# Gate logits of a four-expert block: weights stationary in four column tiles, tokens streaming, and the logits turned back

## What is computed

```python
xn = _modulate(_ln(x), sh_mlp, sc_mlp)                     # 32 x 128 tokens of 144 channels
xf = xn.reshape(-1, C)
gate_logits = xf @ w_gate                                  # w_gate: 144 x 4
topk_logits, topk_idx = jax.lax.top_k(gate_logits, 2)
gates = jax.nn.softmax(topk_logits, axis=-1)
cw = sum(one_hot(topk_idx, 4) * gates[..., None], axis=1)  # token x expert, two of four not zero
hmid = gelu(einsum('tc,ech->eth', xf, w1) + b1)            # all four experts, 576 hidden units each
eo = einsum('eth,ehc->etc', hmid, w2) + b2
moe = einsum('te,etc->tc', cw, eo)
x = x + g_mlp * moe
```

## Time and profile before

| | us |
|---|---|
| median of 3 runs | 1564.3 (1563.18 to 1565.5) |
| span of the profiled execution, first to last instruction | 1547.8 |
| run median less that span | 16.5 |
| TensorE matmul busy | 1415.6 (91%) |
| DVE busy | 1036.5 (67%) |
| ACT busy | 778.5 (50%) |
| POOL busy | 542.2 (35%) |

### The profile page before, as it was taken

How to read it: one execution, slowest core, us unless ns; L and a number is a source line. 1 busy time by engine, 2 the same in 40 slices (tenths; PEclk the granted TensorE clock), 3 DMA queues, 4 the chain that set the end, 5 groups by cost and what they waited for, 6 DMA issues and landing times. The chain is left out here.

```text
span 1547.8 us, 41007 instructions
## 1 busy us (share of the span) xinstructions
PE 1415.6 (91%) x15976; PEld 1065.0 (69%) x15976; DVE 1036.5 (67%) x2592; ACT 778.5 (50%) x1287; POOL 542.2 (35%) x739
## 2 busy tenths in 40 slices
PE   5799988999999998999899778877999799999998
PEld 2377776777777776777676656766777577767776
DVE  4688885766676667888537689887446466666342
ACT  2377763333333335767645456665544266555543
POOL 3355532211131313555323423443335244343322
PEclk9799999999999999999999889999999899999999
DMA  4765631111122032565000333443116667775021
GB/s 129 149 163 147 161 88 52 51 44 44 35 58 75 19 94 62 144 150 138 20 31 22 104 95 104 109 115 104 33 36 86 114 102 109 138 138 97 24 55 47
DMA packets 209128, 134.92 MB, mean 87 GB/s; under 512 B 142461, under 2 KB 191320, under 8 KB 202730
## 3 DMA queue, kind: packets, MB, share of 16 engines
q1 hardware_dynamic: 188978, 129.74, 35.4%
q10 hardware_dynamic: 19960, 2.57, 1.2%
HBM read 98.24 MB, written 33.24 MB: 85 GB/s over the span
## 5 line engine op out<-in xcount | busy, mean ns | idle before, releaser
L1534 DVE TENSOR_REDUCE negm<-banks 128x8 bf16<-128x1024 f32 x256 | 311.1, 1215 | 79.0 <-PE banks L648 77.2
L1223 ACT ACTIVATE prob<-banks 128x1024 f32<-128x1024 f32 x256 | 262.3, 1025 | 194.0 <-PE banks L670 193.3
L1351 ACT ACTIVATE hid<-banks 128x512 f32<-128x512 f32 x144 | 85.9, 597 | 230.5 <-PE banks L951 230.5
L1954 POOL TENSOR_TENSOR X<-X,gx 128x288 f32<-128x288 f32 x128 | 104.7, 831 | 256.9 <-DVE gx L1564 255.1
L967 PEld LDWEIGHTS banks<-wfc,hid 128*128 128x128 f32 x1152 | 157.0, 190 | 30.0 <-issue 19.9
L666 PE MATMUL banks<-qk 54*128 54x128 bf16 (+1 forms) x2048 | 169.4, 236 | 5.7 <-ACT prob L1223 5.0
L670 PE MATMUL banks<-mT,identb 64*128 64x128 bf16 x2048 | 166.2, 225 | 0.3 <-issue 0.3
L967 PE MATMUL banks<-wfc,hid 128*128 128x144 f32 x1152 | 161.4, 286 | 0.0
L648 PE MATMUL banks<-qk 54*128 54x128 bf16 (+1 forms) x2048 | 123.3, 242 | 39.8 <-DVE negm L1534 24.9
L950 PE MATMUL banks<-hT,wfc 128*128 128x512 f32 x288 | 149.1, 599 | 1.7 <-DMA wfc<-in_L_cond_w 1.2
L1725 DVE TENSOR_TENSOR hid<-hid,qk 128x512 f32<-128x512 f32 x128 | 88.9, 695 | 88.8 <-ACT hid L1351 80.4
(11 more groups left out here) (165 smaller groups left out, 2799.2 us busy)
## 6 DMA issues: line engine op xcount, KB each, us to landing
qk<-qk_scr SPq DMA_DIRECT2D x96, 216.0 KB
gbuf<-gate_scr SPq DMA_DIRECT2D x64, 288.0 KB, 4.3
qk_scr<-parts SPq DMA_DIRECT2D x48, 288.0 KB, 2.7
qk<-qk_scr SPq DMA_DIRECT2D x96, 144.0 KB
qk<-cw_scr SPq DMA_DIRECT2D x8, 1024.0 KB, 4.7
qk_scr<-parts SPq DMA_DIRECT2D x48, 144.0 KB, 2.5
qk<-qk_scr SPq DMA_DIRECT2D x96, 72.0 KB
qk<-tok_scr SPq DMA_DIRECT2D x32, 216.0 KB
```

The lines of the kernel that those rows point to most:

```text
L1223: act.activation(prob[:, 2 * (U % 3):2 * (U % 3) + 2, :], pairs[1][:], ACT.Exp, scale=scale).then_inc(a_exp, 1)
L1534: dve.tensor_reduce(negm[:, u // 2, :, 4 * (u % 2):4 * (u % 2) + 4], pairs[0][:].rearrange("q s (h k) -> q s h k", k=T), AX.X, ALU.max, ne ...
L1954: pool.tensor_tensor(x, x, gx[:, q, :, :], ALU.add).then_inc(g_x, 1)
```

## The change

`gate_logits` exchanges the roles of its operands. The four columns of `wgate` become the stationary operand and the 128 tokens of a sequence move. The four sequences' products go to partitions 0, 32, 64 and 96 of the bank, 4 rows and 128 columns each. All four `hT` products are issued first, then the four `hr` products, which now run in float32 over all 66 rows (`rgate` gets two more rows, of zeros).

The logits then have tokens along the columns. A new `logits_out` on DVE copies the bank's 128x128 region to SBUF (`glog`, which reuses the room of `ss`), a new `turn_logits` on TensorE transposes it into columns 128 to 255 of the bank, and `top2` reads there, four of each 32 columns.

The order changes with it. In the expert steps `logits_out` stands at j = 8 and `turn_logits` at j = 9; the parts of `top2` go to j = 10, 11, 12, 14, and `turn_weights` and `copy_weights` to j = 15. In the attention `logits_out` stands at (6, 7), `turn_logits` at (7, 0), and the parts of `top2` at (7, 0), (7, 1), (7, 2), (7, 3); `turn_weights` and `copy_weights` stay at (7, 5) and (7, 6).

```diff
-        rgate = sb("rgate", [REM - 2, E], F32R)
+        rgate = sb("rgate", [REM, E], F32R)
+        glog = ss[:].rearrange("t b h -> t (b h)")
...
                 for b in range(G):
-                    out, at = bank[o][:, E * b:E * b + E], slice(T * b, T * b + T)
-                    pe.matmul(out, hT[:, h, at], wgate[:], start=True, stop=False)
-                    mm = pe.matmul(out, hr[0:REM - 2, h, at], rgate[:], start=False, stop=True)
+                    out, at = bank[o][32 * b:32 * b + E, 0:T], slice(T * b, T * b + T)
+                    pe.matmul(out, wgate[:], hT[:, h, at], start=True, stop=False)
+                for b in range(G):
+                    out, at = bank[o][32 * b:32 * b + E, 0:T], slice(T * b, T * b + T)
+                    mm = pe.matmul(out, rgate[:].bitcast(F32), hr[:, h, at].bitcast(F32), start=False, stop=True)
                 mm.then_inc(s_lg, 1)
+
+            def turn_logits(g, o):
+                pe.wait_ge(d_gl, CR + g + 1)
+                pe.transpose(bank[o][:, T:2 * T], glog[:], ident[:]).then_inc(s_gl, 1)
...
+                        if l == 0 and (g, u) == (7, 0):
+                            turn_logits(0, 6)
...
-                        if g < 7 and j == 14:
+                        if g < 7 and j == 9:
+                            turn_logits(g + 1, 0)
+                        if g < 7 and j == 15:
                             turn_weights(g + 1, 0)
...
-                        if l == 0 and (g, u) in ((6, 7), (7, 0), (7, 1), (7, 3)):
-                            top2(0, {7: 0, 0: 1, 1: 2, 3: 3}[u], 6)
+                        if l == 0 and (g, u) in ((7, 0), (7, 1), (7, 2), (7, 3)):
+                            top2(0, u, 6)
+                        if l == 0 and (g, u) == (6, 7):
+                            logits_out(0, 6)
...
+            def logits_out(g, o):
+                dve.wait_ge(s_lg, CR + g + 1)
+                if g:
+                    dve.wait_ge(s_gl, CR + g)
+                dve.tensor_copy(glog[:], bank[o][:, 0:T]).then_inc(d_gl, 1)
...
-                lv = bank[o][:, 0:G * E].rearrange("t (b e) -> t b e", e=E)
+                lv = bank[o][:, T:2 * T].rearrange("t (b x) -> t b x", b=G)[:, :, 0:E]
...
-                    dve.wait_ge(s_lg, CR + g + 1)
+                    dve.wait_ge(s_gl, CR + g + 1)
...
-                        if g < 7 and j in (9, 10, 11, 13):
-                            top2(g + 1, min(j - 9, 3), 0)
-                        if g < 7 and j == 14:
+                        if g < 7 and j == 8:
+                            logits_out(g + 1, 0)
+                        if g < 7 and j in (10, 11, 12, 14):
+                            top2(g + 1, min(j - 10, 3), 0)
+                        if g < 7 and j == 15:
                             copy_weights(g + 1, 0)
...
+                dve.memset(rgate[REM - 2:REM].bitcast(F32), 0.0)
```

More of the change, by code:

```diff
@@ L265, in build @@
         s_mod, d_ms = sem("s_mod"), sem("d_ms")
+        s_gl, d_gl = sem("s_gl"), sem("d_gl")
         block = ctx.enter_context(nc.Block())
@@ L543, in _ @@
             for x in (s_ada, s_ht, s_hr, s_qk, s_qt, s_v, s_sm, s_mt, s_st, s_pv, s_otok, s_ont, s_onr, s_pj, s_fc1,
-                      s_y, s_lg, s_vt, s_mod, s_k, s_ct):
+                      s_y, s_lg, s_vt, s_mod, s_k, s_ct, s_gl):
                 pe.sem_inc(x, CR)
@@ L1412, in _ @@
             for x in (d_set, d_wa, d_ws, d_mod, d_stat, d_mv, d_hm, d_hr, d_r1, d_sm, d_mt, d_rec, d_on, d_onr, d_gate,
-                      d_ss, d_nw, d_qn, d_top, d_cw, d_y, d_rep, d_xn, d_ms, d_hg, d_bi, d_ct):
+                      d_ss, d_nw, d_qn, d_top, d_cw, d_y, d_rep, d_xn, d_ms, d_hg, d_bi, d_ct, d_gl):
                 dve.sem_inc(x, CR)
@@ L1425, in split_chunk @@
                 st = stage[0:rows, staged(i), 0:n]
-                out = rgate[:] if what == "gate" else SPLIT[what][:, slot(what, k), :]
+                out = rgate[0:rows] if what == "gate" else SPLIT[what][:, slot(what, k), :]
                 dve.wait_ge(d_ws, CR + (i if i < EARLY else i + 1))
```

## The result

The kernel after took 1551.08 us, median of 15 runs (1541.48 to 1557.92); the kernel before took 1563.67 in its 15 runs beside them (1557.37 to 1575.01). The ratio is 0.991, interval 0.9891 to 0.993.

The account below looks back on a forecast made before the run. TensorE was taken to bound the expert layer, a chain of waits the attention's end. 8.9 + 1.0 + 0.4 - 0.4 = 9.9 us off 1564.3 gave 1554.4 us, range 1551.5 to 1560.5.

Parts of the forecast that it names:

- The gate call, 2.05 to 0.65 us: TensorE's gate products: 2.05 us a call before; after, two sets at 0.25 us plus 0.15 for entering the mode.
- The value product of the earlier trace: Attention's float32 product L682 in four column tiles, 0.25 us a set, taken as the price of the new gate products.
- The turn, 0.13 us: The added float32 transpose of the logits on TensorE: 0.13 us a call, bounds 0.1 to 0.3.
- the wait for DVE's copy: TensorE waiting at `turn_logits` for the copy-out: 0.2 us in each of groups 3 and 5, 0.4 in all.
- The `cw` waits of groups 4 and 6, 1.0 us: TensorE's wait at `turn_weights` for DVE's `cw`: 0.5 us goes in each of two groups, bounds 0 and 1.0 in all.
- The late expert weights: Next group's weights read 2.2 us later, 0.4 us left in group 4: nothing charged; slower rival, 1569 us, 4%.
- The first group, +0.4: Gate at the attention's end: 1.2 us saved, nearly all absorbed by DVE waiting for POOL; bounds -1.0 and +1.5.
- the load of the last expert weights under cover: SP's last load of expert weights, behind DVE's `gated` at the attention's end, was said to have cover until 249.56.
- the rival on the clock: The clock fall after the first gate disappears, attention's end gains 1.5 us instead of 0.4: 1552 us; chance 6%.
- The runs lie 16.5 us above that span, and I let that stand: Step from profiled span to run time: the 16.5 us between 1547.8 and 1564.3 were kept unchanged for the new kernel.

Follow-up runs that it names:

- The order alone: The kernel before with only the new order of `top2`, `turn_weights` and `copy_weights`, old gate products kept: 1561.45 us, ratio 0.9991 to before.
- before again: The kernel before, unchanged, run and profiled once more: 1563.33 us, ratio 0.9991 to the other runs of before.
- the first group as before: The kernel after, with the old products and old `top2` places for the first group's gate only: 1554.95 us, ratio 0.9924 to before.
- after again: The kernel after, unchanged, run and profiled once more: 1554.45 us, ratio 0.9946 to before.
- two parts together: The kernel after, with part 2 of the first group's `top2` moved behind part 1 at (7, 1): 1550.58 us, ratio 0.9915 to before.
- old form twice: The kernel before with the 12 instructions of each gate call issued twice: 1596.94 us, ratio 1.0233 to before.
- new form eight times: The kernel after with the 16 instructions of each gate call issued eight times: 1579.85 us, ratio 1.0119 to before.
- four times: The kernel after with the 16 instructions of each gate call issued four times: 1558.73 us, ratio 0.996 to before.
- spread extras: The kernel after with the old products twice more per group, one sequence at each of tiles 10 to 13, result unread: 1580.36 us.

## Why the prediction was right, and where its size was off

**The gate call, 2.05 to 0.65 us: right, but for 0.09 us.** It is 0.55 us to the next product, plus the 0.10 us that this product is slower, plus 0.09 us ahead of the call that the sum did not have: 0.74 in all. The value product of the earlier trace rows was the right row, to 0.03 us a set. The first call, in the attention, took 0.88 us, 0.25 of it an idle stretch. The kernel without column tiles shows the other price, 0.11 us an instruction, to be what it would have been without overlap. The rule of the Trainium skill that was weighed (TensorE: Matmul & The Clock Gate, "Part 3: Packing small matmuls — row/col tiling"), that a weight load overlaps only matmuls of another row group, does not hold here: eight instructions that all use the same rows take 0.22 us in four column tiles and 0.88 us in one. The measurement decides.

**The turn, 0.13 us: right** (0.11, and 0.17 in groups 3 and 5; in group 3 it also starts 0.05 us late, so the wait for DVE's copy is about 0.1 and not the 0.2 that was charged). DVE's copy takes 0.28 us; 0.27 was taken.

**The `cw` waits of groups 4 and 6, 1.0 us: half wrong.** 0.26 us of wait stays in each of them, so the term is 0.5. The order alone shows the same.

**The seven groups together.** The periods of the two first traces, none with a fall, differ by 1.24, 1.19, 1.19, 1.08, 1.42 and 1.08 us, and from the last gate to the last expert product by 1.51 (63.87 and 62.36): 8.7 us, where 8.9 + 1.0 - 0.4 = 9.5 was forecast. The missing 0.8 is the 0.09 at each of seven gates and the half of the `cw` term, less what the turn and the copy waits came out cheaper.

**The late expert weights: nothing lost, right.** In group 4 the read had 0.1 us left of the 0.4 that was worked out.

**The first group, +0.4: too low by luck of the clock, and its chain reached further.** Up to the first weighting nothing was gained: 28.5 us from the gate against 28.2. DVE waits for POOL's `pow` as forecast, 1.70 us where about 2 was said, and `turn_weights` still came 1.2 us earlier after the gate; the `cw_scr` write took that back by landing 3.8 us after its issue and not 2.5. The prediction had the load of the last expert weights under cover. In the traces the write landed right behind that load: at 248.0 and 246.7 in after, at 244.9 and 243.7 in before, and 1.0 to 1.4 us behind it in before again, the order alone, the first group as before, after again, and two parts together as well, where a write of the same size in the expert layer takes 1.3 to 1.4 us. So the loads seem to set this moment; with two parts of `top2` together they were issued 1.4 us earlier after the gate, and the first weighting came 1.8 us earlier. No run moved the loads alone. Behind the first weighting the kernel after made it good. From the first gate to the next, the first traces have 46.20 and 44.88 us, the second ones 46.22 and 45.20: 1.3 and 1.0 us. There the traces of before have two falls and those of after one, and one fall is worth 1.65 us. This is what the rival on the clock said of this place ("gains 1.5 us instead of 0.4"). But the old call without a fall behind it, in the kernel with the first group as before, needed 45.33, so by these traces the change itself is worth 0.1 to 0.5 us here, and the rest is where the falls stood.

So the two traces' difference from the first gate to the last expert product, 8.7 + 1.3 = 10.0 us, meets the forecast's 9.9 because two errors cancel: 0.8 too much in the seven groups, 0.9 too little in the first.

**The step that failed is the one that leaves the clock out of the difference**: "The runs lie 16.5 us above that span, and I let that stand". Those 16.5 us are no constant around the span; a run is its span plus 1.8 to 1.9 us. They are mostly TensorE time at the lower clock, in which the profiled execution of before was lucky (mean clock 0.969; in four later sets of 12 to 31 runs the mean is 0.960 to 0.962), and part of it stands behind gate calls, so it can go with them. The rival on the clock had the right kind of cause, but looked for it only behind the first gate, since the profile shown had no fall behind the other seven.

How much of the gain it is can be estimated from the runs' own clocks. Call 2 x (1 - mean clock) x span the low-clock time of a run; half of it is what the clock costs a kernel that TensorE bounds throughout. Run time less that half is 1493.1 us (standard error 0.9, 15 runs) and 1493.4 (0.9, 11 runs) for after, and 1502.9 (0.8, 31 runs), 1504.2 (1.0, 12), 1502.5 (0.7, 21) and 1501.6 (1.1, 16) for before: on average 1493.2 and 1502.7, so 9.5 us apart, with a standard error of 0.8. The rest is low-clock time: 115.7 us (2.2) in the first 15 runs of after and 121.7 (3.0) in its 11 later ones, against 125.2 (2.0), 120.9 (2.1), 121.5 (1.9) and 117.9 (3.0) in those of before. Averaged over the runs that is 118.2 against 122.1, 4 us less, so 2 us of run time with a standard error of 1.1. Half is an upper price: among runs of one kernel (162 runs in 11 sets), 1 us more of low-clock time goes with 0.39 us of run time (standard error 0.03), perhaps since some of it falls into waits. At that price the steps are 9.9 us and the clock 1.6.

Over all these runs the difference is thus 11.5 us, 9.5 to 9.9 of it the forecast's steps. The first comparison had 12.6, the second 9.6, at 1554.45 us, which lies well inside the predicted range. That the time of 1551.08 fell 0.4 us outside is in part the draw of executions; what the forecast had wrongly at nothing is about 2 us of clock.

That the old calls bring falls and the new ones don't is shown by calls of like length, old form twice and new form eight times: behind seven of seven and behind none. At their own length it is 0, 3 and 2 of seven old calls in the traces of before, before again and the order alone, and 0 of 49 in the seven traces with the new form's call (after twice, the first group as before, four times, eight times, spread extras, two parts together). The three traces have 1.7 falls on average, at 1.65 us each 2.8 us: an estimate from few traces that agrees with the 2 us above within its error. How much of the 12.6 us it was in the runs compared there they don't settle: their clocks are on record for after alone.

**What stays open.** Which trait of the old call brings the clock down was narrowed, not settled. It is not the 4 moving columns alone (five of seven with 128), not the number of instructions in a group (none when spread), and not small products as such (none behind 128 of them in tiles). The calls with falls have in common that the tokens are loaded as the stationary operand, again and again in one place: 5 falls behind 21 calls of 1.95 us, 4 behind 7 of 2.6 us with 66 rows, 7 behind 7 of 4.0 us. The one trace with a call of 1.25 us, also with 66 rows, has none. Length and the change of rows were not varied apart. The loss in the first group's chain by the loads of expert weights was read, not tested.

## What to carry to other kernels

A profile is one execution: before using the distance from its span to the median as a constant, compare its mean clock with that of the runs, and ask which work may bring the clock down in other executions. Where an operand has only a few columns and the other would have to be loaded again for each product, as here, the small one can be made stationary, in four column tiles; without the tiles nothing is gained. And where the old side must stay, giving its second product the same row tile as the first costs a line and gave 0.72 of the 1.20 us here. When TensorE work ahead of a chain of POOL, DVE and DMA gets shorter, place the chain's parts again, or the gain turns into a wait; and look at what else is on the queue ahead of its transfer.

## What the hardware showed that I had not expected

The clock fell while TensorE was busy 100% of the stretch and never waited: behind 0, 3 and 2 of seven calls of 1.95 us in three traces, behind all seven of 4.0 us, and behind none of the same work cut in four and spread over tiles 10 to 13. A fall costs 1.65 us in a period.

The change between products of 128 and of 64 rows costs 0.09 us each time (0.72 us for eight of them in a call) more than the one between 128 and 66 rows.

An 8 KB write issued 1.8 to 2.6 us behind the loads of expert weights landed 1.0 to 1.4 us after the last of them, and took 2.5 to 4.2 us; the same write in the expert layer, with no such loads ahead, takes 1.3 to 1.4.
